# Value products one tile later, another order of the last tiles, and an expert's second product placed inside the next expert's first one

## The reference

```python
x = x + tanh(g_xattn) * attention(layernorm(x), ctx)    # 16 heads of 64, 64 keys, scores masked to own frame
x = x + tanh(g_ffn) * ffn(layernorm(x))
# ffn: probs = sigmoid(x @ gate_w.T); the two best of 16 experts per token
# rank of a token in its expert = number of earlier tokens that chose it; ranks >= 320 are dropped
# h = gelu(rows @ w1[e]);  out = h @ w2[e];  weighted, added to the token's row
```

## Time and profile before

| | us |
|---|---|
| median of 3 runs | 338.72 (338.64 to 340.68) |
| profiled execution, its own time | 339.9 |
| its span in the trace | 338.2 |

### The profile page before, as it was taken

The page is one execution under the profiler, slowest core; times in us unless marked ns, Lnnn a source line. Parts: engine busy times, 40 slices in busy tenths (PEclk is TensorE's granted clock), DMA queues, the critical chain, the costliest instruction groups (busy, mean ns, idle before and its releaser), DMA issues. The chain is left out here.

```text
span 338.2 us, 6265 instructions
## 1 busy us (share of the span) xinstructions
PE 308.3 (91%) x2077; PEld 267.3 (79%) x2080; DVE 251.2 (74%) x585; ACT 207.9 (61%) x570; POOL 191.4 (57%) x242
## 2 busy tenths in 40 slices
PE   8989999999999999998849999999999999999800
PEld 3646779988888888887724899999999999999700
DVE  2679887698989898989755398888888888887200
ACT  2646877887888888866461376666666666665300
POOL 8034566585777777788771023555555555566650
PEclk9999999999999999999978999999999999999965
DMA  6989999700111111111224737878787878853440
GB/s 159 274 241 292 182 167 152 195 19 16 49 49 55 57 57 64 56 51 62 78 95 149 249 104 201 204 205 208 204 216 211 224 202 220 211 82 43 48 46 8
DMA packets 40906, 45.68 MB, mean 135 GB/s; under 512 B 5461, under 2 KB 34666, under 8 KB 40874
## 3 DMA queue, kind: packets, MB, share of 16 engines
q1 hardware_dynamic: 33410, 35.78, 39.3%
q0 software_dynamic: 7424, 9.48, 15.6%
q10 hardware_dynamic: 40, 0.02, 0.0%
HBM read 28.02 MB, written 17.24 MB: 134 GB/s over the span
## 5 line engine op out<-in xcount | busy, mean ns | idle before, releaser
L554 POOL DMA_INDIRECT out_dram<-wqT,diag x48 | 73.3, 1528 | 77.4 <-DMA out_dram<-wqT,diag 43.4
L1370 PE MATMUL ps_scores<-value_t,score_t 128*128 128x320 f32 x384 | 59.1, 310 | 0.0
L1370 PEld LDWEIGHTS ps_scores<-value_t,score_t 128*128 128x128 f32 x384 | 56.5, 188 | 0.4 <-DVE value_t L1079 0.3
L1269 PE MATMUL ps_out<-value_t,pT 128*128 128x256 f32 x384 | 53.3, 289 | 0.9 <-DVE pT L968 0.9
L1240 PE MATMUL ps_scores<-score_t,xn 128*128 128x512 f32 x192 | 53.9, 426 | 0.0
L1269 PEld LDWEIGHTS ps_out<-value_t,pT 128*128 128x128 f32 x384 | 47.7, 189 | 1.7 <-issue 1.6
L1240 PEld LDWEIGHTS ps_scores<-score_t,xn 128*128 128x128 f32 x192 | 36.4, 190 | 6.8
L713 ACT ACTIVATE ps_scores<-ps_scores 128x640 f32<-128x640 f32 x30 | 20.6, 688 | 34.2 <-PE ps_scores L1370 34.1
L460 POOL DMA_INDIRECT padded<-z,slot_row x32 | 33.4, 1043 | 10.0 <-issue 7.1
L640 ACT ACTIVATE probs<-ps_scores,row_low 128x64 f32<-128x64 f32 x128 | 38.0, 327 | 0.5 <-DVE row_low L941 0.5
L1093 DVE CAST value_t<-ps_scores 128x640 fp32r<-128x640 f32 x30 | 24.7, 824 | 18.0 <-ACT ps_scores L713 17.8
(11 more groups left out here) (210 smaller groups left out, 690.0 us busy)
## 6 DMA issues: line engine op xcount, KB each, us to landing
raw<-in_L_ffn_w_dram SPq DMA_DIRECT2D x16, 512.0 KB, 4.8
wo_sb<-in_L_ffn_w_dram SPq DMA_DIRECT2D x16, 512.0 KB, 3.5
padded<-empty SPq DMA_DIRECT2D x2, 2064.0 KB, 31.0
diag<-padded SPq DMA_DIRECT2D x16, 258.0 KB, 4.9
out_dram<-x SPq DMA_DIRECT2D x16, 128.0 KB, 1.7
padded<-empty SPq DMA_DIRECT2D x1, 1032.0 KB, 34.1
diag<-padded SPq DMA_DIRECT2D x16, 64.5 KB, 4.7
wq_sb<-in_L_xattn_Wq_dram SPq DMA_DIRECT2D x2, 512.0 KB, 8.0
```

Of the source, the lines that this page charges most:

```text
L554: pool.indirect_dma_start(out, bass.IndirectOffsetOnAxis(ap=xg[0:SLOTS[k], r, k, TOKEN:TOKEN + 1].bitcast(U32), axis=0), y[0:SLOTS[k], j, ...
L1269: op = pe.matmul(ps_attn, pT[:, a, c], mv, start=c == 0 and (a, b) == PARTS[0], stop=c == HC - 1 and (a, b) == PARTS[-1])
L1370: op = pe.matmul(ps_scores[:, f, 0:CAPACITY], w1_hl(p, a)[:, c, f * P:(f + 1) * P], x_hl(p, b)[:, c], start=c == 0 and (a, b) == PARTS[0], ...
```

## The change

- The attention product of a tile comes three steps after its scores instead of two (`u = s - 1` in all queues), the probabilities have three buffers instead of two (`DEEP`), and the eight value jobs are put after steps -1, 0 and 1.
- The tail now holds tiles 13, 14 and 15. Tiles 13 and 15 use another PSUM bank (`attn_of`) and a second buffer for the transposed probabilities (`pT_of`). The order in all four queues is new; the filler matmuls in it are gone; POOL normalises the last tile instead of DVE; two of the three small operations of `second_norm` go from POOL to DVE and ACT for tiles from 12 on.
- In the experts PE does half of the first product of e+1, the transposes of e+2, the whole second product of e, and then the other half. ACT and DVE take the halves of h in that order, and convert the first weights one step later.
- SP requests the rows first, then the first and the second weights, and in steps from 1 on waits before it until POOL has issued the three scatters of the expert before (`issued`, a memset on POOL each expert).
- Expert 15's second product no longer waits for `y_last` and `y_ready`.

```diff
+LAST = TILES - 1
+DEEP = 3
-        probs = sb("probs", [P, 2, HEADS, KEYS])
+        probs = sb("probs", [P, DEEP, HEADS, KEYS])
+        def attn_of(t):
+            return ps_misc[:, 0:DIM] if t in (LAST - 2, LAST) else ps_out[:, 0:DIM]
+        def pT_of(t, k):
+            return pT_late[:, k] if t in (LAST - 2, LAST) else pT[:, k]
-        JOBS_AFTER = {-2: range(N_FIRST, N_FIRST + 4), -1: range(N_FIRST + 4, N_KEYS + 4), 0: range(N_KEYS + 4, N_JOBS)}
+        VALUES_AFTER = {0: range(N_KEYS + 3, N_KEYS + 5), 1: range(N_KEYS + 5, N_JOBS)}
+        JOBS_AFTER = {-2: range(N_FIRST, N_FIRST + 4), -1: range(N_FIRST + 4, N_KEYS + 3)}
+        def halves(e):
+            if e == -1:
+                return ((0, 0), (0, 1))
+            mine = ((e, 1),) if e > 0 else ()
+            later = ((e + 1, 0),) if 0 <= e < EXPERTS - 1 else ()
+            return mine + later
 # SP, in step e
+                if e >= 1:
+                    sp.wait_ge(issued, e)
+                if e >= -1:
+                    fetch(e + 3)
+                n = e + 4
+                ...                      # first weights of n, then second weights of e + 3
-                if e >= -1:
-                    fetch(e + 3)
 # POOL
+                if t >= LATE_TILE:
+                    pool.tensor_tensor(l2[:, p, 1:2], l2[:, p, 0:1], power[:, 0:1], ALU.pow).then_inc(ln2_ready, 1)
+                    return
+            dispatch(PAIRS - 4, 1, (0,))
+            normalise(LAST)
+            dispatch(PAIRS - 4, 1, (1,))
+            second_norm(LAST - 3)
             mark_tokens(PAIRS - 3)
+            mark_tokens(PAIRS - 2)
             pool.wait_ge(slots_ready, PAIRS - 2)
             dispatch(PAIRS - 3, 0, (0,))
             second_norm(LAST - 2)
             dispatch(PAIRS - 3, 0, (1,))
             dispatch(PAIRS - 3, 1)
-            mark_tokens(PAIRS - 2)
             mark_tokens(PAIRS - 1)
             second_norm(LAST - 1)
             pool.wait_ge(slots_ready, PAIRS - 1)
-            dispatch(PAIRS - 2, 0)
+            dispatch(PAIRS - 2, 0, (0,))
+            second_norm(LAST)
+            dispatch(PAIRS - 2, 0, (1,))
             dispatch(PAIRS - 2, 1)
-            second_norm(LAST)
 # POOL, after the three scatters of expert e
+                if e < EXPERTS - 1:
+                    pool.memset(sent[:, e:e + 1], 0.0).then_inc(issued, 1)
 # ACT, tail
+            copy_probs(LAST - 2)
+            later_exp(LAST, 8, 12)
+            gate_exp(LAST - 4)
+            later_exp(LAST, 12, HEADS)
             copy_probs(LAST - 1)
+            copy_x1(LAST - 3)
+            second_rows(LAST - 4)
+            copy_probs(LAST)
+            gate_exp(LAST - 3)
             copy_x1(LAST - 2)
             second_rows(LAST - 3)
             gate_exp(LAST - 2)
             second_rows(LAST - 2)
-            copy_probs(LAST)
             copy_x1(LAST - 1)
+            gate_exp(LAST - 1)
             second_rows(LAST - 1)
-            gate_exp(LAST - 1)
             copy_x1(LAST)
             ...
 # DVE, tail (new order)
+            low_probs(LAST - 2, 0); low_probs(LAST - 2, 1)
+            row_sum of LAST; first_residual(LAST - 3); second_stats(LAST - 3); row_inv and norm of LAST
+            begin(PAIRS - 3, 0, 2); find(0, 2); choose(PAIRS - 3, 0, 2)
+            low_probs(LAST - 1, 0); low_probs(LAST - 1, 1)
+            weigh(PAIRS - 3, 0, 2); counts_of(PAIRS - 3); place(PAIRS - 3, 0, 2, PAIRS - 2)
+            first_residual(LAST - 2); second_stats(LAST - 2)
+            low_probs(LAST, 0); low_probs(LAST, 1)
+            first_residual(LAST - 1)
+            begin(PAIRS - 2, 0, 2); find(0, 2); second_stats(LAST - 1); choose(PAIRS - 2, 0, 2)
+            weigh(PAIRS - 2, 0, 2); first_residual(LAST)
+            counts_of(PAIRS - 2); place(PAIRS - 2, 0, 2, PAIRS - 1); second_stats(LAST)
+            ...                          # pair 7, tile by tile, as before
 # PE
+                u, ju, iu = s - 1, (j + 1) % 2, (s - 1) // 2
+                if exists(u - 2):
+                    turn_probs(u - 2)
+                ...                      # score(s), turn_x1(u - 3)
+                if s == LAST:
+                    turn_probs(LAST - 2)
+                if exists(u - 2):
+                    attend(u - 2, {HC // 2: lambda: router(u - 3)} if exists(u - 3) else {})
 # PE, tail
             turn_probs(LAST - 1)
-            turn_x1(LAST - 2)
-            keep_busy(5)
-            attend(LAST - 1, {HC // 2: lambda: router(LAST - 2)})
+            attend(LAST - 2, {3: lambda: turn_x1(LAST - 3), HC - 2: lambda: router(LAST - 3)})
+            counts(PAIRS - 3)
             turn_probs(LAST)
+            attend(LAST - 1, {2: lambda: turn_x1(LAST - 2), HC - 2: lambda: router(LAST - 2)})
+            attend(LAST, {2: lambda: turn_x1(LAST - 1), HC - 2: lambda: router(LAST - 1)})
             counts(PAIRS - 2)
-            turn_x1(LAST - 1)
-            keep_busy(3)
-            attend(LAST, {HC // 2: lambda: router(LAST - 1)})
             turn_x1(LAST)
+            router(LAST)
             count_one(0)
-            router(LAST)
             count_one(1)
 # PE, experts
-                    first_product(e, j, i)
+                    first_product(e, j, i, range(FC // 2))
                     turn(e, j, i)
                     second_product(e, j, i)
+                    first_product(e, j, i, range(FC // 2, FC))
```

More of the change, by code:

```diff
@@ L162, in build @@
         l2 = sb("l2", [P, 2, 3])
+        shift = sb("shift", [P, 2, 1])
         eps_c = sb("eps_c", [P, 1])
@@ L499, in step @@
                     split()
[L500 to L504, removed]
+                    if exists(u - 3):
+                        second_norm(u - 3)
+                    if exists(s - 1):
+                        normalise(s - 1)
                 if s == 1:
@@ L539, in _ @@
                 dispatch(PAIRS - 1, k)
-            pool.memset(sent[:, :], 0.0).then_inc(rows_sent, 1)
+            pool.memset(sent[:, EXPERTS - 1:], 0.0).then_inc(rows_sent, 1)
             for k in range(2):
@@ L612, in second_rows @@
                 act.wait_ge(ln2_ready, t + 1)
+                bias = l2[:, p, 2:3]
+                if t >= LATE_TILE:
+                    bias = shift[:, p]
+                    act.activation(bias, l2[:, p, 2:3], ACT.Copy, scale=l2[:, p, 1:2]).then_inc(shifted, 1)
+                    act.wait_ge(shifted, t - LATE_TILE + 1)
                 if t >= RING:
@@ L1071, in _ @@
             choose(PAIRS - 1, 1, 2)
+            weigh(PAIRS - 1, 1, 2)
             counts_of_one(1)
@@ L1259, in attend @@
             def attend(t, between):
-                wait(pe, x1_ready, t)
+                wait(pe, x1_ready, t if t < LAST - 2 else t - 1)
                 for c in range(HC):
@@ L1362, in first_product @@
                     pe.wait_ge(w1_low, t + 1)
-                    for f in range(FC):
+                    for f in fs:
                         if e == -1 and f == FC // 2:
@@ L1379, in second_product @@
                     pe.wait_ge(w2_low, e + 1)
-                    pe.wait_ge(h_low, 2 * e + 2)
+                    pe.wait_ge(h_low, 2 * e + 1)
                     for k in range(SLOT_TILES - 1):
-                        if k == 0:
-                            wait(pe, y_last, e)
-                        else:
-                            wait(pe, y_ready, 2 * e)
+                        if e < EXPERTS - 1:
+                            if k == 0:
+                                wait(pe, y_last, e)
+                            else:
+                                wait(pe, y_ready, 2 * e)
                         for f in range(FC):
+                            if k == 0 and f == FC // 2:
+                                pe.wait_ge(h_low, 2 * e + 2)
                             for a, b in PARTS:
```

265 lines of the change are left out of this document (137 added, 128 removed).

## The result

The changed kernel takes 337.19 us (median of 20 runs, 336.17 to 338.82), the kernel before 338.87 (20 runs, 337.99 to 362.15): ratio 0.9948, interval 0.9937 to 0.996, **0.5% faster** where 0.2% slower was forecast. The profiled execution took 337.04 us, span 335.1; before it was 339.9 and 338.2. So the two traces lie 2.9 us apart (3.1 in span) and the medians 1.7, because the profiled run of before was 1.0 above its own median. Some single runs were disturbed (two of the kernel before here, and the profiled one of e1, span 351.3); the ratios leave them out, the lists and medians of runs don't.

What follows compares the result with a forecast made beforehand. It took PE to bound the loop, a chain through DVE and POOL the tail, and POOL's scatters and landing waits the experts' end. Terms -2.3 - 0.4 + 7.0 - 3.6 = +0.7 gave median 339.4 us, eight in ten 334.8 to 344.2.

Steps and rivals of the forecast that it cites:

- First product of the experts: 188.69 moves with the last scatter.: Between tail and experts: the experts' first product shifts by as much as POOL's last scatter of the tail.
- Start of the loop: Attention loop, steps 0 to 3: step 4 begins at 58.0 against 60.33, -2.3 us, bounds -4.2 and -1.5.
- The stall at 76.62: Attention loop: PE's wait for POOL's normalisation gets a step more of slack, -0.4 us, bounds -0.45 and 0.
- The tail: After step 15 began: last scatter issued at 37.7 us against 30.7, +7.0, bounds +5.0 and +8.0.
- Slots of pair 6: Tail, DVE's routing queue: ready 26.6 us after step 15 began, against 18.5 before.
- The experts: Expert stage: POOL scatters expert 15's first result at 320.3 instead of 324.07; -3.6 us taken, bounds -4.9 and +4.
- The sum: Whole kernel: -2.3 - 0.4 + 7.0 - 3.6 = +0.7 us, span 338.9, median 339.4.
- The faster one: Rival, loop and tail: DVE's order costs less, idle below 0.5 us before pair 6's slots; 335 to 335.5 us; chance 0.24.
- The slower one: Rival, experts: POOL's landing wait grows above 3.0 us, period 8.55, +6.8 in all, 345.5 us; chance 0.13.
- No gain from the order of requests: Rival, experts: place among SP's requests is indifferent, waits stay at 2.9 us, +4.3, 343.0 us; chance 0.13.

Runs made afterwards that it cites:

- e1: The kernel before with 23 instead of 40 filler matmuls ahead of the transposes of expert 0's rows: 341.74 us, ratio 0.999.
- e15: The kernel before with 30 instead of 40 filler matmuls: 339.63 us, ratio 1.0007.
- e2: The changed kernel with 34 instead of 40 filler matmuls: 337.4 us, ratio to the kernel before 0.9936.
- e7: The changed kernel with 50 instead of 40 filler matmuls: 340.76 us, ratio to the kernel before 1.0017.
- e8: The changed kernel with pair 6's slots placed ahead of the last tile's residual on DVE, and 32 fillers: 336.3 us, ratio to the kernel before 0.9906.
- e11: e8 with POOL's factor of the last tile behind both first scatters of pair 6 instead of between them: 335.87 us, ratio to the kernel before 0.9892.
- e5: The changed kernel without SP's wait for `issued`, rows still asked for first: 337.43 us, ratio to the kernel before 0.9948.
- e6: The changed kernel with SP's old order of requests and no wait for `issued`: 340.31 us, ratio to the kernel before 1.0011.
- e14: The changed kernel with the old order of products on PE, DVE and ACT, and no wait for `issued`: 352.68 us, ratio to the kernel before 1.0407.
- e13: The changed kernel with the old order of products on PE, DVE and ACT; requests and wait as changed: 340.25 us, ratio to the kernel before 1.0036.
- e3: The kernel before with only the experts' part of the change (products, requests, `issued`): 338.82 us, ratio 0.9977.
- e4: The changed kernel with the experts as before, so the attention part (loop and tail) alone: 341.92 us, ratio to the kernel before 1.0105.
- e12: The kernel before with the experts' part of the change alone and 30 fillers instead of 40: 336.1 us, ratio 0.9898.

## Why the prediction was wrong

**The step that failed: "First product of the experts: 188.69 moves with the last scatter."** It was given one sentence and no row. The forecast had the last scatter 4.3 us later than before (-2.3 - 0.4 + 7.0) and moved the experts by as much. Measured: the last scatter 2.2 later, the first product 0.1. The first product waits for the later of two things, the fillers' end and the landing of the rows, and before the change the fillers' end was the later by 2.2 to 2.6 us: the transposes started 5.99 us after the request for the rows (186.18 less 180.19), and with fewer fillers, waiting for the rows, they start 3.35 (e1) and 3.82 (e15) after it. e1, e2, e7 and e15 show it from both sides. The rows at 186.18 and 180.12 stood in the trace: no wait ahead of the transposes meant that the landing didn't set them. The forecast took that stretch for DMA latency. Of the 4.2 us that this term had too much, 2.1 are this step; the other 2.1 are the sizes of loop and tail, which follow. With all its other sizes as they were, and this step put right, the forecast would have been -1.5 to -1.9 instead of +0.7.

**Start of the loop**, -2.3 forecast, -3.2 measured, inside the bounds; over all traces the means differ by 2.5. PE shows waits of 0.49, 0.52 and 0.65 us there, not 0.65, 1.1, 1.0 and 0.5: the places were right, the waits half as long. The stall at 76.62 went, but was worth 0.1 and not 0.4: from step 4 to step 15 it is 87.24 us instead of 87.36.

**The tail**, +7.0 forecast, +5.4 measured (36.1 less 30.7), inside its bounds. Slots of pair 6 at 25.4 instead of 26.6: DVE's low part of tile 13 began at 6.5 instead of 7.1, and its work took about 1 us less than the 18.3 added up. The rest, 11.1 forecast and 10.7 measured. The chain was the right one: counted from step 4's start e8 has the last scatter 0.25 us earlier and e11 0.71. Whether the slower clock of the tail (0.82, 0.89 in the earlier trace rows) cost something wasn't tested; DVE waits 1.01 us for a product of PE in it.

**The experts**, -3.6 forecast, -3.1 measured from the first product on. Expert 0's first scatter at 198.99 (forecast 198.9), expert 1's at 207.15 (206.9), then a period of 8.21 set by PE. Missed: the last first result at 320.28 instead of 319.9, and 0.8 us instead of 0.4 from it to the scatter, which is what POOL takes behind a result elsewhere too. (The parts named for three scatters, two of 1.56, one of 1.42 and two gaps, make 5.14 us and not 5.24; nothing hangs on it.) The reason given was that the requests come behind the scatters. Their place fits: in e5 they lie there without the wait and it has the same time, in e6 the second weights don't and it is 0.6% slower, in e14 all lie beside the first two scatters and it is the slowest. But place isn't all: e13 has the same waiting as the changed kernel and is 0.9% slower, with scatters of 2 us, and the short first landing comes in e6 with the old order of requests. Why single scatters take some 2 us, in e13 and also in e3 and e7 with the new products, stays open.

**The sum** by the traces: 0.1 - 3.1 = -3.0, where the two profiled executions differ by 2.9 (3.1 in span); the medians differ by 1.2 less than that, since the kernel before was profiled above its median. The forecast knew that and carried its +0.7 over to the median, but its -3.6 was read from the very stage, paced by landings, in which executions of that kernel differ.

**Rivals.** The faster one (DVE's order costs less) named a wrong place, though part of it is in the 5.4: DVE's idle time before pair 6's slots, which was to be below 0.5 us, was 2.1 (0.67, 0.43 and 1.01). The slower one didn't come: no wait above 2.95 us. "No gain from the order of requests" is refuted by e5 against e6. Its rule of the Trainium skill (DMA: Bandwidth & Descriptors, queues, rings and completion order: a DMA engine takes turns between queues with work) fits e14, where loads beside scatters go with waits of up to 5.04 us, but it doesn't tell when the two meet, and that decided here.

## What to carry over

Before moving a late stage's start by a delay, look at what ends last in front of it: an instruction without idle time before it (here behind 40 filler matmuls) isn't waiting for the thing one has in mind, and filler work tuned for one chain hides a delay of 2 us in it. When a chain of transfers and an engine's pace lie close together (8.02 and 8.21 us an expert here), the order of requests on another queue and the order of products count together: test them as a grid, since one alone may lose 3% (e14 against e4). And orders written by hand on three engines are one order.

## What the runs showed of the hardware

- The same fillers take different times: 11.3 us for 40 in the changed kernel, 9.4 for 32 in e11, 8.3 for 30 in e12 and 12.0 for the 49 recorded of 50 in e7. In the kernel before the last 28 took 6.21 us (0.22 each, granted clock 1.00, 2.4 GHz), the 11 ahead of them 4.86 (0.44 each, granted clock 0.50, 1.2 GHz). The clock rises at another filler in each execution; the granted clock of 175 to 186 us was 0.74 (e11) to 0.86 (e12) in these five.
- POOL's scatter takes 1.57 us, and sometimes up to 2.4 (e6, e7, e13, e14). In e7 experts paced by PE turned at such a one into experts paced by landings, which cost 2.2 us (124.30 against 122.11); that it was the cause isn't shown.
- Some kernels paced by PE repeat within about 1 us (e2 336.54 to 337.63, e11 335.40 to 336.11, six runs each), and e3 and e7 scatter by 4 to 5; but e5, paced by PE in its trace, also has runs of 339.50 and 341.14 above a lowest of 336.60.
